# First expert units placed anew in a language-model tower; the attention's squares transposed on TensorE and summed by heads on VectorE

## The reference, cut to what matters

```
Y = jnp.einsum('bnst,bntd->bnsd', A, V)          # per head, d = 32
m = Y.mean(-1, keepdims=True)
v = ((Y - m) ** 2).mean(-1, keepdims=True)
Yn = ((Y - m) / jnp.sqrt(v + EPS)).reshape(...) * gnw + gnb
return G * jax.nn.sigmoid(G) * Yn @ WO
```

```
idx = jnp.argmax(xf @ Wg + bg, axis=-1)
for e in range(8):
    y = relu(xf @ W1[e] + b1[e]) @ W2[e] + b2[e]
    out = jnp.where((idx == e)[:, None], y, out)
```

## Time and profile before

| what | value |
|---|---|
| median of 3 runs | 2424.34 us |
| profiled execution: its time | 2426.54 us |
| profiled execution: span of the core | 2424.7 us |
| granted TensorE clock, mean over the span | 0.978 |
| TensorE matmul busy | 2234.7 us (92%) |
| VectorE busy | 1885.7 us (78%) |
| ScalarE busy | 1582.2 us (65%) |
| GpSimd busy | 1763.2 us (73%) |

### The profile page before, as it was taken

One profiled execution on the slowest core, in us unless ns is written; L12 is line 12 of the kernel. 1 busy time (PEld: TensorE's weight loads), 2 busy tenths in 40 slices (PEclk: granted clock), 3 DMA queues, 4 the chain that ended last, 5 costly groups with the idle time before them and its releaser, 6 DMA issues.

```text
span 2424.7 us, 52857 instructions
## 1 busy us (share of the span) xinstructions
PE 2234.7 (92%) x18308; PEld 1949.5 (80%) x18309; DVE 1885.7 (78%) x5669; ACT 1582.2 (65%) x5066; POOL 1763.2 (73%) x1762
## 2 busy tenths in 40 slices
PE   1589999999999999999999999999999999996885
PEld 0368888888888888888888888888888888885774
DVE  5757888888787888888888888887878888865653
ACT  0256677776767676776777767767676776763663
POOL 5687677777777777778787777777777774334677
PEclk9799999999999999999999999999999999998997
DMA  3111011111011111111011111111111111002332
GB/s 123 28 46 33 24 41 29 39 29 42 26 41 27 36 33 36 34 34 37 27 42 26 43 27 41 29 40 28 37 31 35 34 29 56 15 13 61 93 106 71
DMA packets 63523, 98.12 MB, mean 40 GB/s; under 512 B 19108, under 2 KB 41126, under 8 KB 63152
## 3 DMA queue, kind: packets, MB, share of 16 engines
q0 software_dynamic: 33216, 67.44, 10.3%
q1 hardware_dynamic: 30064, 27.53, 4.0%
HBM read 76.63 MB, written 19.17 MB: 40 GB/s over the span
## 4 chain that ended last, share of the span: by engine, by line
PE 75%; POOL 9%; DVE 8%; issue 4%; ACT 3%; DMA 1%; DVEq 0%; SPq 0%; POOLq 0%; ACTq 0%
PE psum L1511 65%; PE psum L1532 7%; POOL both_grams L772 3%; PE psum L1585 3%; POOL gr L807 2%; POOL out L826 2%; DVE hid L1287 2%; ACT qm L909 1%; ACT qkT L907 1%; ACT xn L920 1%; DVE side_n L1238 1%; DVE qk L1266 0%; POOL rstd L783 0%; DVE hid L1263 0%; DVE qk L1262 0%
## 5 line engine op out<-in xcount | busy, mean ns | idle before, releaser
L772 POOL DMA_INDIRECT both_grams<-gram_table,idx_all x768 | 779.0, 1014 | 188.3 <-issue 182.8
L1511 PE MATMUL psum<-xT,lw 128*128 128x256 f32 x1920 | 482.5, 385 | 0.0
L807 POOL TENSOR_TENSOR gr<-ms,con 128x8 f32<-128x8 f32 x192 | 319.1, 1662 | 138.2 <-DVE ms L1292 133.5
L1511 PE MATMUL psum<-lw,hid 128*128 128x129 f32 x3072 | 390.9, 276 | 2.4 <-ACT hid L939 2.4
L1511 PEld LDWEIGHTS psum<-lw,hid 128*128 128x128 f32 x3072 | 370.7, 192 | 12.2 <-issue 6.0
L783 POOL TENSOR_TENSOR rstd<-ss,con 128x2 f32<-128x2 f32 x320 | 234.2, 734 | 197.5 <-ACT squares L883 195.4
L1511 PEld LDWEIGHTS psum<-xT,lw 128*128 128x128 f32 x1920 | 341.7, 193 | 32.6
L939 ACT ACTIVATE hid<-psum,par 128x256 f32<-128x256 f32 x768 | 307.7, 487 | 44.9 <-PE psum L1511 42.3
L1511 PE MATMUL psum<-lw,xT 128*128 128x256 f32 (+1 forms) x1536 | 290.2, 332 | 6.5 <-ACT xT L895 6.5
L895 ACT ACTIVATE xT<-psum,par 128x256 f32<-128x256 f32 x384 | 213.9, 561 | 120.2 <-PE psum L1532 119.1
L1511 PEld LDWEIGHTS psum<-lw,xT 128*128 128x128 f32 x1536 | 251.7, 193 | 33.6 <-ACT xT L895 7.2
(11 more groups left out here) (244 smaller groups left out, 4742.6 us busy)
## 6 DMA issues: line engine op xcount, KB each, us to landing
both_grams<-gram_table,idx_all POOLq DMA_INDIRECT x768
xb<-x SPq DMA_DIRECT2D x32, 256.0 KB, 3.3
idx_all<-routed_rows SPq DMA_DIRECT2D x20, 132.0 KB
er<-routed_rows SPq DMA_DIRECT2D x20, 132.0 KB
both_grams<-routed_rows SPq DMA_DIRECT2D x20, 132.0 KB
qm<-routed_rows SPq DMA_DIRECT2D x20, 132.0 KB
both_grams<-expert_w SPq DMA_DIRECT2D x8, 321.0 KB, 5.5
lw<-layer_w SPq DMA_DIRECT2D x1, 2503.5 KB, 11.6
```

The costliest lines, as they stand in the source:

```text
L772: pool.indirect_dma_start(grams[s][:, g, c, :], None, gram_table, bass.IndirectOffsetOnAxis(ap=idx_all[:, g, at:at + 1], axis=0))\
L807: pool.tensor_tensor(gr[s][:, c], ms[s][:, c], const("half")[:, 0:n], ALU.pow).then_inc(y_r[s], 1)
L1511: return pe.matmul(dst, lhsT, rhs, start=start, stop=stop)
```

## The change

1. **Squares.** `act sq` squares y/sqrt(32) + sqrt(EPS/32) instead of y, with a bias read from a new column of constants (`root_eps`). As a head's y sums to zero, 32 such squares sum to mean square + EPS. `pe ms` transposes the two chunks of `sq` (two transposes instead of two products with 4 columns), and `dve ms` sums 32 neighbours (a reduction of 128 x 256 numbers to 128 x 8).
2. **First units.** `turn`, `up`, `up_weights`, `copy_T`, `relu` and `normed` of the fourth unit move into `first_unit`; GpSimd stores three units' rows there; the due times in `FIRST_UNIT` are others, most of them earlier. `normed(0, 0)` waits until TensorE has read `xn[0]` for the last time. On TensorE the experts' numbers are read before `up` or before the unit's `turn` instead of right before `down`, and the waits for them move ahead of `up(0, 0)`.
3. **Behind the main program** VectorE's order changes: `result(0, 3)` before `biased(1, 0)`; `tiles_left` before it too; `schedule` is cut into `tiles_before` and the rest, and both stand ahead of `normed(1, 2)`.
4. **Orders.** Many entries of `AT` and `FIRST_AT` move by fractions of a us, a few by more. In a pair of the middle (pair 7) the order that results differs from before in about seven places on TensorE, five on VectorE, four on ScalarE and none on GpSimd, each a step that passes one or a few neighbours. `LATER_GATHERS` changes one entry by 0.09.

```diff
 FIRST_UNIT = {
-    "turn": (17.1, 26.95, 36.45), "up": (22.9, 31.9, 44.4), "down": (27, 36.4, 56.2),
-    "up_weights": (11, 11.1, 31), "copy_T": (16.4, 27.9, 37.4), "relu": (21.5, 30.9, 52.9),
-    "normed": (16.15, 24, 40.6), "biased": (18.9, 24.9, 50.8), "result": (35.6, 44.7, 64.5),
-    "rows": (37.5, 50.8)}
+    "turn": (12.4, 18.4, 36.45, 56.1), "up": (15.8, 27, 44.4, 56.2), "down": (22.9, 32.4, 49.6),
+    "up_weights": (9.9, 10, 31, 51.4), "copy_T": (11.4, 20.4, 37.4, 52.8), "relu": (16.4, 27.9, 48.4, 53),
+    "normed": (7.4, 17.4, 31.4, 51), "biased": (16.4, 30, 45.9), "result": (24.4, 36.4, 50.9),
+    "rows": (28.4, 38.4, 58.4)}
...
-    "act norm1_T": ((0.42, 1.94, -0.3), (1.29, 0, 3.24), (0.42, 1.94, -0.3), (1.29, 0, 3.24)),
+    "act norm1_T": ((1.4716, 1.94, -0.3), (1.29, 0.0, 3.24), (0.42, 0.6825, -0.0232), (1.29, 0.0, 3.24)),
...
+    c[:, CONST["root_eps"]] = (EPS / HD) ** 0.5
...
             def first_unit():
-                for j in range(2):
+                for j in range(3):
                     yield FIRST_UNIT["rows"][j]
...
-            for j in range(2, SETS):
-                pool.wait_ge(e_ys, nth(0, SETS, j + 2))
-                store_rows(j)
+            pool.wait_ge(e_ys, nth(0, SETS, SETS + 1))
+            store_rows(SETS - 1)
...
-                act.activation(sq[s][:, CS[h], :], chunks(bank_a(s, h))[:, 0:2, :], ACT.Square)
+                act.activation(sq[s][:, CS[h], :], chunks(bank_a(s, h))[:, 0:2, :], ACT.Square,
+                               bias=const("root_eps"), scale=float(HD) ** -0.5)
...
-                dve.tensor_scalar(ms[s][:, h * n:(h + 1) * n], a[:, 2 * P:2 * P + n], 1.0 / HD, EPS, ALU.mult, ALU.add)\
-                   .then_inc(y_ms[s], 1)
+                dve.tensor_reduce(ms[s][:, h * n:(h + 1) * n], a[:, 2 * P:].rearrange("p (n d) -> p n d", d=HD),
+                                  axis=AX_X, op=ALU.add).then_inc(y_ms[s], 1)
...
                 dve.sem_inc(e_ys, 2)
                 yield FIRST_UNIT["normed"][0]
+                dve.wait_ge(xT_p[0][1], pairs * NORMS)
                 normed(0, 0)
...
-            normed(0, 3)
             biased(0, 3, first=True)
             normed(1, 0)
+            result(0, 3, first=True)
+            tiles_left()
             biased(1, 0)
-            result(0, 3, first=True)
             normed(1, 1)
+            tiles_before()
             biased(1, 1)
-            tiles_left()
+            schedule()
             normed(1, 2)
-            schedule()
             dve.wait_ge(s_hash_f, SCHEDULED)
...
-                for c in half_chunks(h):
-                    last = mm(a[:, 2 * P + c % 2 * HEADS:2 * P + (c % 2 + 1) * HEADS], sq[s][:, c, :],
-                              const("heads").rearrange("p (n d) -> p n d", d=HD)[:, :, 0])
-                last.then_inc(ms_p[s], 1)
+                half_transposes(a[:, 2 * P:], sq[s], h).then_inc(ms_p[s], 1)
...
                 yield FIRST_UNIT["up"][0]
+                pe.wait_ge(s_hash_f, FIRST_TILES)
+                pe.wait_ge(e_w, 16 * E)
+                first = experts(0, 0)
+                pe.wait_ge(x_s[0], nth(pairs * LAYERS - 1, 2, 1))
                 up(0, 0)
+                second = experts(0, 1)
                 yield FIRST_UNIT["turn"][1]
                 turn(0, 1)
                 yield FIRST_UNIT["down"][0]
-                pe.wait_ge(s_hash_f, FIRST_TILES)
-                pe.wait_ge(e_w, 16 * E)
-                down(0, 0)
+                down(0, 0, first)
...
+                yield FIRST_UNIT["turn"][3]
+                turn(0, 3)
+                yield FIRST_UNIT["up"][3]
+                up(0, 3)

             main_program(embed, attend, feed, route, first_unit=first_unit)
-            turn(0, 3)
-            up(0, 3)
             turn(1, 0)
             down(0, 3)
```

More of the change, by code:

```diff
@@ L55 @@
     "pool rstd2": ((1.21, 3.35, 0.76), (2.66, 0.99, 0.49), (1.21, 3.35, 0.76), (2.66, 0.99, 0.49)),
[2 rows of a table removed]
[L58 removed]
[8 rows of a table removed]
[L67 removed]
[6 rows of a table removed]
[L74 to L76 removed]
[2 rows of a table added]
+    "act qkT": ((-12.08, 10.24, 7.54), (8.14, 11.51, 6.74), (-13.0471, 10.24, 7.54), (8.14, 11.51, 6.74)),
[8 rows of a table added]
+    "dve rope": ((6.8452, 8.28, 5.9258), (6.37, 7.95, 8.8634), (7.8901, 8.28, 5.56), (6.37, 9.1339, 8.85)),
[6 rows of a table added]
+    "act spread": ((21.25, 23.28, 21.07), (24.25, 21.09, 19.3147), (21.25, 23.28, 21.07), (24.25, 21.09, 20.25)),
+    "pe rT_y": ((24.08, 23.76, 23.24), (24.0612, 23.7721, 21.9843), (23.6693, 23.76, 23.24), (23.19, 24.2397, 21.95)),
+    "pool gr": ((24.5218, 21.59, 25.23), (24.31, 22.36, 18.9109), (24.97, 22.5414, 25.23), (24.31, 22.36, 19.74)),
     "pool rstd0": ((54.68,), (57.78,), (54.68,), (57.78,)),
@@ L115 @@
     "pool rstd1": ((-145.21, 1.48, 0.25), (32.6, 0.79, 0.07), (-145.21, 1.48, 0.25), (32.6, 0.79, 0.07)),
[3 rows of a table removed]
-    "act qkT": ((-12.08, 10.24, 7.54), (8.14, 11.51, 6.74), (-12.08, 10.24, 7.54), (8.14, 11.51, 6.74)),
[8 rows of a table removed]
-    "dve rope": ((6.97, 8.28, 5.56), (6.37, 7.95, 8.85), (6.97, 8.28, 5.56), (6.37, 7.95, 8.85)),
[4 rows of a table removed]
[3 rows of a table added]
+    "act qkT": ((-12.08, 10.24, 7.54), (8.14, 11.51, 6.9901), (-14.0404, 10.24, 7.54), (8.14, 11.51, 6.8219)),
[8 rows of a table added]
+    "dve rope": ((6.97, 8.28, 5.56), (6.37, 7.95, 9.0151), (6.97, 8.28, 5.56), (7.0902, 7.95, 8.85)),
[4 rows of a table added]
@@ L155 @@
-    "pool scatter": ((98.58,), (102.17,), (98.58,), (102.17,)),
-    "act accT": ((26.42,), (27.37,), (26.42,), (27.37,)),
-    "act h0": ((43.68,), (43.22,), (43.68,), (43.22,)),
-    "act ss0": ((60.62,), (60.89,), (60.62,), (60.89,)),
-    "act rT": ((22.83,), (33.64,), (22.83,), (33.64,)),
-    "dve onehot": ((1.4,), (5.36,), (1.4,), (5.36,)),
-    "dve acc2": ((3.43,), (-101.47,), (3.43,), (-101.47,)),
[5 rows of a table added]
+    "pool scatter": ((98.5052,), (102.17,), (98.5052,), (102.17,)),
+    "act accT": ((26.42,), (27.37,), (26.42,), (27.37,)),
@@ L162 @@
+    "act h0": ((43.68,), (60.56,), (43.68,), (43.22,)),
+    "act ss0": ((41.58,), (60.89,), (60.62,), (63.32,)),
+    "act rT": ((22.83,), (33.4934,), (25.5635,), (35.0417,)),
+    "dve onehot": ((1.4,), (5.36,), (2.53,), (5.36,)),
+    "dve acc2": ((3.43,), (-101.47,), (2.02,), (-101.47,)),
     "dve acc4": ((9.97,), (7.68,), (9.97,), (7.68,)),
-    "dve mom0": ((49.01,), (50.98,), (49.01,), (50.98,)),
+    "dve mom0": ((48.8,), (50.98,), (49.01,), (50.98,)),
     "dve x0": ((55.73,), (61.84,), (55.73,), (61.84,)),
-    "dve row": ((3.29,), (3.34,), (3.29,), (3.34,)),
@@ L166 @@
-    "dve rn": ((18.99,), (12.1,), (18.99,), (12.1,)),
+    "dve row": ((3.29,), (3.8217,), (3.29,), (3.34,)),
+    "dve rn": ((18.99,), (12.1,), (18.99,), (10.9004,)),
     "dve pick": ((45.26,), (46.24,), (45.26,), (46.24,)),
-    "dve slot": ((62.46,), (66.06,), (62.46,), (66.06,)),
+    "dve slot": ((62.46,), (66.8465,), (62.46,), (66.06,)),
     "pe accT": ((23.67,), (25.55,), (23.67,), (25.55,)),
     "pe h0": ((40.43,), (42.85,), (40.43,), (42.85,)),
-    "pe rT": ((23.68,), (32.7,), (23.68,), (32.7,)),
@@ L172 @@
-    "pe logits": ((43.09,), (43.68,), (43.09,), (43.68,)),
-    "pe places": ((59.05,), (59.99,), (59.05,), (59.99,)),
+    "pe rT": ((23.68,), (32.7,), (23.68,), (32.7657,)),
+    "pe logits": ((44.8479,), (43.9414,), (43.09,), (43.9414,)),
+    "pe places": ((59.05,), (59.99,), (59.05,), (60.0695,)),
 }
@@ L202 @@
     ("before", P), ("gram_scale", NG), ("beyond", NG), ("vocab", 1), ("byte", 1), ("token", CH), ("rank", E),
-    ("region", E), ("half", 16), ("tile", 80), ("gram_row", NG),
+    ("region", E), ("half", 16), ("root_eps", 1), ("tile", 80), ("gram_row", NG),
     ("parity", 2)])
@@ L981, in first_unit @@
                 up_weights(0, 1)
-                for j in range(3):
+                for j in range(2):
                     yield FIRST_UNIT["copy_T"][j]
@@ L986, in first_unit @@
                     relu(0, j)
-                    if j == 1:
-                        yield FIRST_UNIT["up_weights"][2]
-                        up_weights(0, 2)
+                yield FIRST_UNIT["up_weights"][2]
+                up_weights(0, 2)
+                yield FIRST_UNIT["copy_T"][2]
+                copy_T(0, 2)
+                yield FIRST_UNIT["relu"][2]
+                relu(0, 2)
+                yield FIRST_UNIT["up_weights"][3]
+                up_weights(0, 3)
+                yield FIRST_UNIT["copy_T"][3]
+                copy_T(0, 3)
+                yield FIRST_UNIT["relu"][3]
+                relu(0, 3)
             main_program(embed, attend, feed, route, first_unit=first_unit)
-            copy_T(0, 3)
-            up_weights(0, 3)
-            relu(0, 3)
             copy_T(1, 0)
@@ L1407, in tiles_left, with tiles_before @@
                 link(dve.tensor_tensor(cnt[0:1, 3, :], cnt[0:1, 1, :], taken[0:1, 1:E + 1], ALU.subtract))
-            def schedule():
```

(15 more changed lines are left out.)

40 lines of the change are left out of this document (21 added, 19 removed), and 108 rows, old and new, of tables (AT, FIRST_AT).

## The result

Six runs of the changed kernel: median 2435.16 us (2434.66 to 2436.49), beside 2425.73 us for six of the kernel before on the same chip. The ratio is 1.0041, interval 1.0031 to 1.0051: 9.9 us slower, on the other side of the forecast and outside its range. The profiled execution took 2436.46 us, its span 2434.7.

What follows compares the result with a forecast made beforehand. TensorE (98.7% busy) was taken to bound the middle, GpSimd's stores the last 157 us. First sum -23 and second -12 made -35 on 2426.5, 2391.5; the runs' median lies 2.2 lower: forecast 2389 us, range 2375 to 2411.

Steps and rivals of the forecast that it cites:

- The prediction's estimate by that page's figure, +34 us: Squares on TensorE: at 275 ns a transpose, a pair costs 0.55 us, not 0.36; first sum +34 instead of -23.
- the chain's 2 us: Half's chain from y to z: 0.20 us longer, mostly hidden by other streams; 2 of the 25 us saved given up.
- GpSimd's waits of 1.73 and 1.35 us: Behind round 1's first store: GpSimd's waits, 3.1 us together, of which 2 us were to go.
- the sentence on the head sum: Sum on VectorE: +0.25 us per half, 48 us more work, hidden by VectorE's idle time.
- The transposes' term of -25: Squares on TensorE: 0.14 us less per half over 180 halves, 25 us less TensorE work; bounds 18 and 29.
- The first sum: Middle of the kernel: the squares' transposes less the chain's part, -23 us.
- (c): Rival: the middle gives half, as gaps between TensorE's records take back savings; 2400 us, chance 0.06.
- (e): Rival: VectorE takes the pace, TensorE pays its +48 us and gets 25 back; +23 - 12, 2435 us, chance 0.06.
- The due times: New due times move only a few neighbours past each other: priced at nothing, between 6 us lost and 6 gained.
- The 6.6 us: Last pair: shorter norm wait (2), full clock (1.3) and two stalls gone (1.3, 2.0), 6.6 us gained.
- the term of 3.5 us: Behind the main program: VectorE's shorter wait for `result(0, 3)` brings round 1's first result 3.5 us earlier.
- Second sum: End of the kernel: last pair, order behind the main program and GpSimd's later waits, -12 us; 4 to 18 gained.

Runs made afterwards that it cites:

- e9: e1 without the square's bias, so that EPS is left out of the norm: 2427.38 us, ratio 1.0008.
- e5: Kernel before with the squares transposed on TensorE, but VectorE's old step of 8 columns (head sum left out) and no bias: 2409.88 us, ratio 0.9934.
- e7: Kernel before with an additional VectorE reduction of 176 constants per half right behind the head sum's step, outside the half's chain: 2432.58 us, ratio 1.0028.
- e6: Kernel before with an additional VectorE reduction of 176 constants per half ahead of the head sum's step, inside the half's chain: 2439.24 us, ratio 1.0056.
- e1: Kernel before with part 1 of the change (squares) alone, all orders as before: 2428.28 us, ratio 1.0013.
- e11: e2 with the fourth unit's steps behind the main program again: 2425.72 us, ratio 1.0002.
- e10: e2 with VectorE's old order behind the main program, the schedule still cut in two: 2420.67 us, ratio 0.9981.
- e14: The changed kernel with VectorE's old order behind the main program, as in e10: 2427.37 us, ratio 1.0010.
- e2: Kernel before with parts 2 and 3 of the change alone (first units, order behind the main program): 2428.14 us, ratio 1.0011.
- e8: e1 with GpSimd's root on 4 of each half's 8 numbers, the other norms using 1: 2411.67 us, ratio 0.9939.
- e16: Kernel before with squares and head columns in bf16, new first units except the fourth, VectorE's old order behind the main program: 2395.07 us, ratio 0.9873.

## Why the prediction was wrong

**What held.** The clock at 1.00, VectorE's share, the slot of the transposes, `dve ms` at 0.42 us and `act sq` at 0.47 came as worked out. On the page "TensorE: Matmul & The Clock Gate" of the Trainium skill, Part 4: its rule that a transpose doesn't count as a busy TensorE for the clock cost nothing here, where 384 more transposes stand among many products and the clock stayed at 1.00 for 1800 us. The page's 275 ns for a transpose is what the record shows (278 ns), not what the queue pays (0.21 to 0.25 us for two). The prediction's estimate by that page's figure, +34 us, left out the chain's 2 us and should read +36. The bias was as good as hidden. GpSimd's stores at 1.30 us set the last stretch in every run, and GpSimd's waits of 1.73 and 1.35 us behind the first store of round 1, of which the forecast took 2 us away, are gone in the changed kernel: from that store to the last one it is 162.5 us, 165.2 before.

**The step that failed in the middle** is this one, in the half's own chain: "Four streams share TensorE, and while one waits, another's step is next, so most of it is hidden. Of the 25 us I let 2 go for this", together with the sentence on the head sum, "It is hidden by VectorE's idle time". Both terms stood at 2 us together, and the sum on VectorE measured 18 (e9 against e5). e7 shows VectorE's load costing 6.8 us for 63.6 with 17% of the engine idle, e6 the same again for its place in the chain. The order of each engine is fixed, so a step that comes late isn't passed by another stream's: it holds the queue. And TensorE's 98.7% was read as if only this engine's work counted. Its records run on into the next group's (a pair of transposes is recorded with 0.38 us and its follower starts after 0.25), so a wait shorter than the tail of a record doesn't show as idle time. The transposes' term of -25 was itself too large: e5 gives -16, and its waits for `xn` grew from 12.9 to 24.4 us. The first sum, forecast -23, measured +3.2 (e1). Of the rivals, (c), in which gaps between the records take back half of the saving, is not far from e5, but has no price for the sum; (e) has the sign, but at +3 and not +23: VectorE doesn't take the pace, it shares it with the chain and with TensorE. That the total is (e)'s 2435 is luck: it comes from other terms, the due times and the end.

**The due times** were priced at nothing, within 6 us either way. That is within those bounds: with the new operations they cost 3.2, nearly all in pair 0, whose length the prediction never looked at as TensorE works little there; little work of TensorE's there doesn't make the order of its steps free. Which of its due times is at fault wasn't looked for.

**The last pair.** The 6.6 us were right for the three units that were accounted (e11), the match to a tenth by luck: of the mark's 6.6 us, 0.4 were there before the last `gr` step. In the changed kernel TensorE's wait of 3.15 us is down to 1.33 us ahead of `up(0, 0)` and 0.96 behind it, and the first feed-forward product takes 1.97 us instead of 3.32. The fourth unit was dismissed with "Work that moves in: `turn(0, 3)` and `up(0, 3)`, 2.2 us of TensorE in a stretch with 22.6 us of idle time". The wait of 4.13 us wasn't named, nor who stands behind `turn(0, 3)` while it waits for `normed(0, 3)`: the last stream's logits.

**Behind the main program** the term of 3.5 us had the wrong sign, and the step that failed is "With `up(0, 3)` done early that wait shrinks to some 2 us", with the sentence behind it by which `normed(1, 1)` and `normed(1, 2)` only gain less through what now stands ahead of them. VectorE's wait for `result(0, 3)`, 7.76 us before, is still 5.45 in the changed kernel and 4.63 in e10. What stands ahead of the two delays them by 4.7 and 7.6 us (against e14), not only by the 2.6 and 2.7 of the sums, and TensorE's clock over this stretch is 0.67 instead of 0.78. Second sum: forecast -12, measured +2.7 (e2), of which the order is +7.3 and the rest -4.6.

**Not settled.** Why the sum on VectorE costs 18 us where e6, cut to its length, gives 10; how e8's gain divides between the chain and GpSimd. Signalling the squares ahead of the `zp` copy wasn't tried, since TensorE would then write a bank that ScalarE still reads; due times made for e16 weren't tried either.

## What to carry to other kernels

A busy share of 98% doesn't say that only this engine's work counts. Put the same small operation once into the suspected chain and once beside it: the difference prices the chain, and the second run prices the engine. When steps move into a fixed order, ask of each what it waits for and what is queued behind it; here 2.2 us of work that waited for 4 put the steps behind it back by 5. And orders made for one set of lengths can cost a lot when the lengths are others, here 16.5 us.

## What the runs showed of the hardware

A 128x4 product of f32 costs TensorE's queue 0.18 us (0.36 for two), more than a transpose of 128x128 in f32 (0.11 to 0.12); in bf16 two such products take 0.05 us. GpSimd's root took 1.66 us on 8 numbers per row and 1.03 on 4. A bias read from memory adds 0.09 us to a 128x256 square on ScalarE.
